# Fused cross-attention and feed-forward layer: a row of query factors through DRAM in place of four matmuls a batch, and the positions made ahead of x's low halves

## The chip, the cores and the metric

One core of a Trainium2 chip runs the whole kernel. The metric is the device time of one execution in microseconds (us), as a median over runs; lower is better.

## What is computed

```python
def _layernorm(x, axis=-1, eps=1e-05):
    ...
    x = x + _L0_xattn_ref(_layernorm(x, axis=-1), ctx_1024, ctx_1024, mask, fside, Wq, bq, Wk, bk, Wv, bv, Wo, bo)
    x = x + _L0_ffn_ref(_layernorm(x, axis=-1), W1, W2, ln_g, ln_b, router_W, router_b, raw_U, raw_V, gamma)
...
    q = _split_heads(Q @ Wq.T + bq)
    k = _split_heads(K @ Wk.T + bk)
    v = _split_heads(V @ Wv.T + bv)
    scores = jnp.einsum('bhqd,bhkd->bhqk', q, k) / jnp.sqrt(jnp.float32(DK))
    scores = jnp.where(mask == 0, jnp.float32(-1000000000.0), scores)
    scores = scores + attn_bias
    probs = jax.nn.softmax(scores, axis=-1)
```

Batch 8, 512 tokens of 512 features for x and for the context, 16 heads of 32, hidden width 2048, all float32. The mask is int32, 512x512 a batch.

## The kernel before

The kernel has three stages, each a block with a program of its own for each engine: `project` (L131) makes queries, keys, values and positions of all eight batches and splits the feed-forward weights, `attend` (L513) does the attention, `blend` (L875) the rest. At the end of a block all engines meet. The change is in `project` alone, which covers about the first 312 of 1888 us.

To keep precision at the fast rate of the matmul, each matrix is kept as a high half (rounded) and a low half (what is left), and each product is three passes (`PASSES`, L26), so one output tile of 128x512 takes 4 chunks x 3 passes = 12 matmuls of 128x512. A batch has 12 such products: four for k, four for v, four for q. They go through four PSUM banks (`ps_j`, `NPB = 4`), in this order on TensorE (L467 to L508): four k products, then 16 transposes of the normalised x (`xn`) into three banks (`ps_t`; the fourth group of four reuses the first bank and waits until VectorE has made the low half of the first, `xT_low`, L490), then four v products, then four small matmuls that spread the query factors over all partitions, then four q products. Each k product of the next batch reuses the bank of a q product, and waits until VectorE has read that (`bank_free`, L471).

The query factor is, for each query token, -1/sqrt(32), or 0 where the token's whole row of the mask is 0. VectorE makes the positions (1e9 where the mask is 0, L381), their minimum over each row (L384), and from it `q_fac` (L388): 128 partitions x 4. The q tiles have features on the partitions and tokens along the row, so the factors are wanted as a row of 512 that is the same on all partitions. Before, VectorE spreads each column to 128x128 (`fac_cols`, L392), TensorE multiplies these by the identity (L503) into a bank of its own (`ps_f`), and ScalarE copies that to `fac_row` (L450), which L410 reads when it moves q out of PSUM with bias and factor.

VectorE's order in a batch: statistics of x (L363, L367, L369), `xn` (L372, with `rstd` from GpSimd, L330), the four low halves `xT_l` (L376, each after ScalarE's high half, L445), positions, minimum, `q_fac`, `fac_cols`, four v tiles (L399), the low half of the next context (L356), four q tiles (L410).

SyncE issues all loads and stores of the stage on one queue, in the order of L263 to L299, and each wait holds back everything behind it: the feed-forward weights, the next context and x, the store of k, the store of the positions, the next mask, v, q, and the split weights. GpSimd makes the low half of the weights (L334, L339) and `rstd`. In batch 0 it does one such pass more, for the output projection's weights (L334).

Of the kernel before, what the change touches and what calls it, by code (L numbers as in the profile page):

```python
# [17 lines left out]
P = 128  # L18
# [25 lines left out]
def build(nc, x, ctxT, bias, mask, WqT, bq, WkT, bk, WvT, bv, WoT, bo, W1T, W2T,  # L44
          ln_g, ln_b, rWT, rb, rawU, rawV, gamma, out):

    q_d, k_d = (nc.dram_tensor(n, (NC * B, P, S), F32, kind="Internal").ap() for n in ("q_d", "k_d"))
    v_d = nc.dram_tensor("v_d", (NC * B, S, P), F32, kind="Internal").ap()
    pos_d = nc.dram_tensor("pos_d", (B, S, S), F32, kind="Internal").ap()
    att_d = nc.dram_tensor("att_d", (NC * B, P, S), F32, kind="Internal").ap()  # L50
    wo_d = nc.dram_tensor("wo_d", (2, P, NC * D), F32, kind="Internal").ap()
    wf_d = nc.dram_tensor("wf_d", (NF, P, 4, D), F32, kind="Internal").ap()

    with ExitStack() as top:
        ident = top.enter_context(nc.sbuf_tensor("ident", [P, P], F32))
        ones = top.enter_context(nc.sbuf_tensor("ones", [P, P], F32))
        neg_half = top.enter_context(nc.sbuf_tensor("neg_half", [P, NT], F32))
        ahead = Ahead(nc, top)
        project(nc, ident, ones, neg_half, x, ctxT, mask, WqT, bq, WkT, bk, WvT, bv, W1T, W2T,
                q_d, k_d, v_d, pos_d, wf_d, bias, WoT, wo_d, ahead)  # L60
        kept = Kept(nc, top)
        attend(nc, ident, bias, q_d, k_d, v_d, pos_d, att_d, x, wo_d, bo, rawU, rawV, kept, ahead)
        blend(nc, ident, ones, neg_half, x, att_d, ln_g, ln_b, rWT, rb, gamma, wf_d, kept, ahead, out)
# [65 lines left out]


def project(nc, ident, ones, neg_half, x, ctxT, mask, WqT, bq, WkT, bk, WvT, bv, W1T, W2T,  # L131
            q_d, k_d, v_d, pos_d, wf_d, bias, WoT, wo_d, ahead):
    NPJ = 3 * NC
    NPB = 4
    NTB = 3
    with ExitStack() as ctx:
        def sb(name, shape, dt=F32):
            return ctx.enter_context(nc.sbuf_tensor("p_" + name, shape, dt))

        def sem(name):  # L140
            return ctx.enter_context(nc.semaphore("p_" + name))
# [13 lines left out]
        pos = sb("pos", [P, NT, S])  # L155
        pos_min = sb("pos_min", [P, NT])
        q_fac = sb("q_fac", [P, NT])
        fac_cols = sb("fac_cols", [P, NT, P])
        fac_row = sb("fac_row", [P, S])
        bq_c, bk_c = sb("bq_c", [P, NC]), sb("bk_c", [P, NC])  # L160
        bv_r = sb("bv_r", [P, D])
# [5 lines left out]

        ps_t = ctx.enter_context(nc.psum_tensor("p_ps_t", [P, NTB, S], F32))
        ps_j = ctx.enter_context(nc.psum_tensor("p_ps_j", [P, NPB, D], F32))
        ps_f = ctx.enter_context(nc.psum_tensor("p_ps_f", [P, S], F32))  # L170

        consts_made = sem("consts_made")
        consts_zeroed = sem("consts_zeroed")
# [1 line left out]
        x_in, c_in, m_in = sem("x_in"), sem("c_in"), sem("m_in")  # L175
        kw_in, vw_in, qw_in = sem("kw_in"), sem("vw_in"), sem("qw_in")
        w_high, w_low = sem("w_high"), sem("w_low")
        pos_done, min_done, fac_done, cols_done = sem("pos_done"), sem("min_done"), sem("fac_done"), sem("cols_done")
        stats_done, mv_done, var_done, rstd_done, xn_done = (
            sem("stats_done"), sem("mv_done"), sem("var_done"), sem("rstd_done"), sem("xn_done"))  # L180
        x_turned, xT_high, xT_low = sem("x_turned"), sem("xT_high"), sem("xT_low")
        cT_high, cT_low = sem("cT_high"), sem("cT_low")
        fac_turned, fac_row_done = sem("fac_turned"), sem("fac_row_done")
        wf_in, wf_high, wf_low, wf_out = sem("wf_in"), sem("wf_high"), sem("wf_low"), ahead.wf_out
        wo_in, wo_high, wo_low, wo_out = sem("wo_in"), sem("wo_high"), sem("wo_low"), sem("wo_out")
        projected, bank_free = sem("projected"), sem("bank_free")
# [22 lines left out]
        def _(sp):  # L209
# [53 lines left out]
            def body(b, more):  # L263
                if b > 0:
                    sp.wait_ge(wf_low, b)
                    load_ff(b)
                if b >= B - 3:
                    load_ahead(b - (B - 3))
                if more:
                    sp.wait_ge(cT_low, b + 1)  # L270
                    load_c(b + 1)
                    sp.wait_ge(xn_done, NT * (b + 1))
                    load_x(b + 1)
                sp.wait_ge(k_done, NC * (b + 1))
                store_qk(b, k_s, k_d, k_out)
                sp.wait_ge(pos_done, b + 1)
                sp.dma_start(tokens(pos_d[b]), pos[:, :, :]).then_inc(pos_out, 16)
                if more:
                    load_m(b + 1)
                if b == 0:  # L280
                    sp.wait_ge(wo_low, 1)
                    store_wo()
                    load_ff(b)
                sp.wait_ge(bank_free, NPB + NVQ * b + NT)
                for c in range(NC):
                    sp.dma_start(tokens(v_d[B * c + b]), v_s[:, :, c * P:(c + 1) * P]).then_inc(v_out, 16)
                if more:
                    sp.wait_ge(bank_free, NPB + NVQ * (b + 1))
                    store_qk(b, q_s, q_d, q_out)
                else:  # L290
                    for c in range(NC):
                        if c == NC // 2:
                            sp.wait_ge(wf_low, b + 1)
                            store_ff(b)
                        sp.wait_ge(bank_free, NPB + NVQ * b + NT + c + 1)
                        sp.dma_start(q_d[B * c + b], q_s[:, c, :]).then_inc(q_out, 16)
                if more:
                    sp.wait_ge(wf_low, b + 1)
                    store_ff(b)  # L299
# [45 lines left out]
        def _(dve):  # L345
# [13 lines left out]
            def body(b, more):  # L359
# [11 lines left out]
                for t in range(NT):  # L371
                    dve.tensor_scalar(xn[:, t, :], x_raw[:, t, :], mv[:, t, 0:1], rstd[:, t:t + 1],  # L372
                                      ALU.subtract, ALU.mult).then_inc(xn_done, 1)
                for c in range(NC):
                    dve.wait_ge(xT_high, NC * b + c + 1)
                    dve.tensor_tensor(out=xT_l[:, c, :], in0=ps_t[:, c % NTB, :], in1=xT_h[:, c, :].bitcast(F32),  # L376
                                      op=ALU.subtract).then_inc(xT_low, 1)

                dve.wait_ge(m_in, 16 * b + 16)
                dve.wait_ge(pos_out, 16 * (b + 1))  # L380
                dve.tensor_scalar(pos[:, :, :], m_raw[:, :, :], 0.0, MASKED, ALU.is_equal, ALU.mult) \  # L381
# [5 lines left out]

                dve.tensor_scalar(q_fac[:, :], pos_min[:, :], 0.0, QSCALE, ALU.is_equal, ALU.mult) \  # L388
                    .then_inc(fac_done, 1)
                dve.wait_ge(fac_done, b + 1)  # L390
                for t in range(NT):
                    dve.tensor_scalar(fac_cols[:, t, :], ones[:, :], q_fac[:, t:t + 1], None, ALU.mult) \  # L392
                        .then_inc(cols_done, 1)
                for t in range(NT):
                    n = V_AT + t
                    dve.wait_ge(projected, NPJ * b + n + 1)
# [3 lines left out]
                        .then_inc(bank_free, 1)  # L400
                if more:
                    context_low(b + 1)
                dve.wait_ge(fac_row_done, b + 1)
                for c in range(NC):

                    n = Q_AT + c
# [16 lines left out]
        def _(act):  # L423
# [9 lines left out]
            def body(b, more):  # L433
# [12 lines left out]
                if more:  # L446
                    act.wait_ge(projected, NPJ * b + V_AT + NT)
                    context_high(b + 1)
                act.wait_ge(fac_turned, b + 1)
                act.activation(fac_row[:, :], ps_f[:, :], ACT.Copy).then_inc(fac_row_done, 1)  # L450
                act.wait_ge(wf_in, 64 * (b + 1))
                act.wait_ge(wf_out, 64 * (b + 1))
                act.wait_ge(wo_out, 32)
# [10 lines left out]
        def _(pe):  # L464
            pe.wait_ge(consts_made, 3)

            def body(b, more):  # L467
# [29 lines left out]
                for t in range(NT):  # L497
                    ts = slice(t * P, (t + 1) * P)
                    product(V_AT + t, [(a[:, k, ts], w[:, k, :]) for k in range(NC)
                                       for a, w in ((cT_h, w_h[2]), (cT_h, w_l[2]), (cT_l, w_h[2]))])  # L500
                pe.wait_ge(cols_done, NT * (b + 1))
                for t in range(NT):
                    last = pe.matmul(ps_f[:, t * P:(t + 1) * P], fac_cols[:, t, :], ident[:, :], start=True, stop=True)  # L503
                last.then_inc(fac_turned, 1)
                pe.wait_ge(w_low, 3)
                pe.wait_ge(xT_low, NC * (b + 1))
                for c in range(NC):
# [1030 lines left out]
```

## Time and profile before

| | us |
|---|---|
| median of 3 runs | 1891.92 (1888.12 to 1892.15) |
| profiled execution | 1890.4 |
| its span | 1888.5 |
| TensorE busy | 1818.5 (96%) |
| VectorE / ScalarE / GpSimd busy | 1037.1 / 793.8 / 888.1 |
| DMA queue of SyncE | 50.7% of 16 engines' span |

The span is what the trace covers; the execution lies 1.9 us above it. Times in the trace are us from the span's start. Rows of an engine's timeline give start, length, engine, line, operation, output<-inputs, and in brackets how long the engine sat idle before and what released it. PE is TensorE, DVE VectorE, ACT ScalarE, POOL GpSimd, SPq SyncE's queue. A matmul's length overlaps the next one's; from start to start, two matmuls of 128x512 are some 0.23 us apart.

### The profile page before, as it was taken

What the parts mean: (1) busy time and instruction counts of PE and PEld (TensorE: products, weight loads), DVE (VectorE), ACT (ScalarE), POOL (GpSimd) and SP (SyncE); (2) the same over time, 40 slices, a digit from 0 to 9 for tenths busy, and PEclk for the clock granted to TensorE, in tenths of its full rate; (3) what the DMA queues carried; (4) which work ended last, traced back from release to release, by engine and by line L of the source; (5) the groups of instructions that cost most, each with busy time, mean ns of one, the idle gap of its engine ahead of it and who ended that gap; (6) DMA issues with size and microseconds to landing.
All of it is one profiled execution on the core that took longest, in us unless ns stands there. A gap on an engine that the chain in (4) does not pass through costs nothing.

```text
span 1888.5 us, 31571 instructions
## 1 busy us (share of the span) xinstructions
PE 1818.5 (96%) x11736; PEld 1358.6 (72%) x11736; DVE 1037.1 (55%) x2401; ACT 793.8 (42%) x1720; POOL 888.1 (47%) x702
## 2 busy tenths in 40 slices
PE   6999998999999999999699999999999999999998
PEld 5888886555555555555477888888888888888886
DVE  5555555998998999899654422433233342332411
ACT  3222223888888888888331211312112131221310
POOL 1211214999999999999213232232322413223211
PEclk9999998999999999999889999999999999999999
DMA  8888888626245335431433463554535555355453
GB/s 298 286 302 313 311 314 310 244 96 224 91 135 178 137 115 174 147 115 36 143 116 101 150 213 123 179 189 163 195 122 189 188 170 190 121 198 177 150 188 114
DMA packets 198007, 340.11 MB, mean 180 GB/s; under 512 B 10464, under 2 KB 52064, under 8 KB 197344
## 3 DMA queue, kind: packets, MB, share of 16 engines
q1 hardware_dynamic: 194592, 325.50, 50.7%
q0 software_dynamic: 3264, 12.58, 1.9%
q8 instruction: 96, 1.57, 0.3%
q14 instruction: 55, 0.45, 0.1%
HBM read 268.84 MB, written 69.21 MB: 179 GB/s over the span
## 4 chain that ended last, share of the span: by engine, by line
PE 49%; DVE 2%; ACT 1%; issue 0%; POOL 0%; DVEq 0%; ACTq 0%
PE n_ps_y L1459 18%; PE n_ps_h L1440 18%; PE n_ps_m L1376 9%; PE n_ps_y L1376 2%; PE n_ps_m L1370 1%; DVE n_aT_l L1080 0%; DVE h_bias L1180 0%; DVE n_stats L1093 0%; DVE h_k L1180 0%; DVE h_bias L1152 0%; DVE n_g_h L1234 0%; DVE k_az L1105 0%; DVE k_x L1226 0%; DVE h_k L1161 0%; POOL n_rstd L1043 0%
## 5 line engine op out<-in xcount | busy, mean ns | idle before, releaser
L1062 POOL TENSOR_TENSOR n_g_l<-h_pos,n_g_h 128x512 fp32r<-128x512 f32 x128 | 186.4, 1456 | 581.3 <-DVE n_g_h L1234 581.3
L863 ACT ACTIVATE a_t_s<-a_t_s,a_nmax 128x512 f32<-128x512 f32 x512 | 364.4, 715 | 15.8 <-DVE a_nmax L812 15.8
L1440 PE MATMUL n_ps_h<-n_zT_h,n_w 128*128 128x512 f32 x1024 | 338.5, 392 | 2.1 <-DVE n_r_row L1210 2.1
L812 DVE CUSTOM_DVE_ANT_0 a_t_s<-a_ps_s,a_t_s 128x512 f32<-128x512 f32 x464 | 295.2, 687 | 44.8 <-PE a_ps_s L722 27.9
L733 PEld LDWEIGHTS a_ps_t<-ident,a_t_s 128*128 128x128 f32 x2048 | 221.3, 142 | 136.7 <-issue 108.8
L694 POOL TENSOR_TENSOR a_t_s<-a_pos,a_bias_t 128x512 f32<-128x512 f32 x256 | 317.8, 1271 | 0.2
L1459 PE MATMUL n_ps_y<-n_w,n_g_h 128*128 128x512 f32 x1024 | 316.6, 390 | 0.0
L1332 ACT ACTIVATE h_pos<-n_ps_h 128x512 f32<-128x512 f32 x128 | 75.5, 596 | 535.4 <-PE n_ps_h L1440 535.4
L733 PE MATMUL a_ps_t<-ident,a_t_s 128*128 128x128 f32 x2048 | 281.6, 281 | 0.3 <-ACT a_pT L850 0.3
L1234 DVE CAST n_g_h<-h_pos 128x512 fp32r<-128x512 f32 x128 | 55.8, 436 | 374.2 <-ACT h_pos L1332 374.2
L1440 PEld LDWEIGHTS n_ps_h<-n_zT_h,n_w 128*128 128x128 f32 x1024 | 193.3, 189 | 42.5 <-DVE n_r_row L1210 2.5
L1459 PEld LDWEIGHTS n_ps_y<-n_w,n_g_h 128*128 128x128 f32 x1024 | 191.2, 188 | 39.0
L1440 PE MATMUL n_ps_h<-n_zT_l,n_w 128*128 128x512 f32 x512 | 200.1, 391 | 0.0
L1459 PE MATMUL n_ps_y<-n_w,n_g_l 128*128 128x512 f32 x512 | 199.4, 389 | 0.0
L850 ACT ACTIVATE a_pT<-a_ps_t 128x512 f32<-128x512 f32 x256 | 151.4, 592 | 75.1 <-PE a_ps_t L733 75.0
L819 DVE COPY a_pT<-a_ps_t 128x512 f32<-128x512 f32 x256 | 164.3, 683 | 1.8 <-PE a_ps_t L733 1.8
L722 PE MATMUL a_ps_s<-h_k,h_q 32*128 32x512 f32 x1024 | 147.0, 643 | 16.5 <-DVE a_nmax L812 10.1
L747 PE MATMUL a_ps_o<-a_pT,a_v 128*32 128x256 f32 x2048 | 149.9, 388 | 0.0
L339 POOL TENSOR_TENSOR p_wf_l<-p_wf,p_wf_h 128x2048 fp32r<-128x2048 f32 x8 | 37.0, 4624 | 186.0 <-ACT p_wf_h L454 186.0
L694 POOL TENSOR_TENSOR a_t_s<-a_pos,h_bias 128x512 f32<-128x512 f32 x96 | 119.6, 1270 | 0.0
L1440 PEld LDWEIGHTS n_ps_h<-n_zT_l,n_w 128*128 128x128 f32 x512 | 96.7, 189 | 19.9
L1459 PEld LDWEIGHTS n_ps_y<-n_w,n_g_l 128*128 128x128 f32 x512 | 96.1, 188 | 20.1
(165 smaller groups left out, 2652.1 us busy)
## 6 DMA issues: line engine op xcount, KB each, us to landing
n_w<-wf_d SPq DMA_DIRECT2D x256, 512.0 KB, 4.2
a_pos<-pos_d SPq DMA_DIRECT2D x24, 1024.0 KB, 6.3
a_bias_t<-in_bias POOLq DMA_DIRECT2D x9, 1024.0 KB, 7.2
p_c_raw<-in_ctxT SPq DMA_DIRECT2D x8, 1024.0 KB, 8.0
p_x_raw<-in_x SPq DMA_DIRECT2D x8, 1024.0 KB, 10.3
p_m_raw<-in_mask SPq DMA_DIRECT2D x8, 1024.0 KB, 12.7
k_d<-p_k_s SPq DMA_DIRECT2D x8, 1024.0 KB, 12.1
pos_d<-p_pos SPq DMA_DIRECT2D x8, 1024.0 KB, 10.5
```

What stands on the lines that cost most here:

```text
L694: pool.tensor_tensor(out=t_s[:, j % NN, i:i + 1, :], in0=pos_rows(b, qt, qt + 1), in1=bias_rows(i, i + 1, qt), op=ALU.subtract).then_inc(n ...
L722: pe.matmul(ps_s[:, i, :], q[rows, b, qt * P:(qt + 1) * P], k[rows, b, :], start=True, stop=True).then_inc(scored, 1)
L733: last = pe.transpose(ps_t[:, BANK[i], kt * P:(kt + 1) * P], t_s[:, at[1] % NN, i, kt * P:(kt + 1) * P], ident[:, :])
L747: last = pe.matmul(ps_o[rows, :], v[:, b, kt, rows], pT[:, h, i, kt, :], start=kt == 0, stop=kt == NT - 1)
L812: dve.tensor_tensor_reduce(t_s[:, j % NN, i:i + 1, :], ps_s[:, i:i + 1, :], added, 1.0, 3.0e38, ALU.add, ALU.min, nmax[:, j % NN, i:i + 1] ...
L819: dve.tensor_copy(dst, src).then_inc(kept_dve, 1)
L850: act.activation(dst, src, ACT.Copy).then_inc(kept_act, 1)
L863: act.activation(t_s[:, j % NN, i, :], t_s[:, j % NN, i, :], ACT.Exp, scale=-1.0, bias=nmax[:, j % NN, i:i + 1], accum_out=total[:, j // 2 ...
L1062: pool.tensor_tensor(out=g_l[:, f % NG, :], in0=g_f[:, f % NG, :], in1=g_h[:, f % NG, :].bitcast(F32), op=ALU.subtract).then_inc(g_low, 1)
L1376: last = pe.matmul(dst, stationary, moving, start=start and n == 0, stop=stop and n == len(passes) - 1)
L1440: last = pe.matmul(ps_h[:, f % 2, :], stationary, moving, start=i == 0, stop=i == len(passes) - 1)
L1459: last = pe.matmul(ps_y[:, t, :], gs[i], w2[:, f % NW, j, :], start=f == 0 and m == 0, stop=f == NF - 1 and m == 2)
```

## The change

The factors go to DRAM and come back. A tensor `fac_d` (8 x 512) is added. SyncE stores `q_fac` into it, 512 single elements of 4 bytes, waits for that store, and loads the row of 2 KB to all 128 partitions as `fac_row`. `fac_cols`, its four VectorE operations, the four matmuls, the bank `ps_f` and ScalarE's copy go. On VectorE the positions, the minimum and `q_fac` come ahead of `xT_l`. On SyncE the positions' store, the factor store and the next mask's load come ahead of the store of k, and the factor load, with its waits, behind it.

```diff
@@ tensors of project
-        fac_cols = sb("fac_cols", [P, NT, P])
-        ps_f = ctx.enter_context(nc.psum_tensor("p_ps_f", [P, S], F32))
...
@@ SyncE, body of a batch
                     load_x(b + 1)
+                sp.wait_ge(pos_done, b + 1)
+                sp.dma_start(tokens(pos_d[b]), pos[:, :, :]).then_inc(pos_out, 16)
+                sp.wait_ge(fac_done, b + 1)
+                sp.dma_start(fac_d[b].rearrange("(t p) -> p t", p=P), q_fac[:, :],
+                             allow_slow_non_contiguous=True).then_inc(fac_out, 16)
+                if more:
+                    load_m(b + 1)
                 sp.wait_ge(k_done, NC * (b + 1))
                 store_qk(b, k_s, k_d, k_out)
-                sp.wait_ge(pos_done, b + 1)
-                sp.dma_start(tokens(pos_d[b]), pos[:, :, :]).then_inc(pos_out, 16)
-                if more:
-                    load_m(b + 1)
+                sp.wait_ge(fac_out, 16 * (b + 1))
+                sp.wait_ge(bank_free, NPB + NVQ * b)
+                sp.dma_start(fac_row[:, :], fac_d[b].rearrange("(a n) -> a n", a=1).broadcast_to([P, S])) \
+                    .then_inc(fac_in, 16)
                 if b == 0:
@@ VectorE, body of a batch
                                       ALU.subtract, ALU.mult).then_inc(xn_done, 1)
-                for c in range(NC):
-                    dve.wait_ge(xT_high, NC * b + c + 1)
-                    dve.tensor_tensor(out=xT_l[:, c, :], in0=ps_t[:, c % NTB, :], in1=xT_h[:, c, :].bitcast(F32),
-                                      op=ALU.subtract).then_inc(xT_low, 1)
-
                 dve.wait_ge(m_in, 16 * b + 16)
...
                     .then_inc(fac_done, 1)
-                dve.wait_ge(fac_done, b + 1)
-                for t in range(NT):
-                    dve.tensor_scalar(fac_cols[:, t, :], ones[:, :], q_fac[:, t:t + 1], None, ALU.mult) \
-                        .then_inc(cols_done, 1)
+                for c in range(NC):
+                    dve.wait_ge(xT_high, NC * b + c + 1)
+                    dve.tensor_tensor(out=xT_l[:, c, :], in0=ps_t[:, c % NTB, :], in1=xT_h[:, c, :].bitcast(F32),
+                                      op=ALU.subtract).then_inc(xT_low, 1)
+
...
-                dve.wait_ge(fac_row_done, b + 1)
+                dve.wait_ge(fac_in, 16 * (b + 1))
@@ ScalarE, body of a batch
-                act.wait_ge(fac_turned, b + 1)
-                act.activation(fac_row[:, :], ps_f[:, :], ACT.Copy).then_inc(fac_row_done, 1)
@@ TensorE, body of a batch
-                pe.wait_ge(cols_done, NT * (b + 1))
-                for t in range(NT):
-                    last = pe.matmul(ps_f[:, t * P:(t + 1) * P], fac_cols[:, t, :], ident[:, :], start=True, stop=True)
-                last.then_inc(fac_turned, 1)
```

VectorE's order from `xn` to the v tiles, the same in each batch. Before:

```order
L372 TENSOR_SCALAR p_xn<-p_x_raw,p_mv,p_rstd 128x512 x3
L376 TENSOR_TENSOR p_xT_l<-p_ps_t,p_xT_h 128x512 [waits p_xT_high] x4
L381 TENSOR_SCALAR p_pos<-p_m_raw 128x2048 [waits p_pos_out,p_m_in]
L384 TENSOR_REDUCE p_pos_min<-p_pos 128x4 [waits p_pos_done]
L388 TENSOR_SCALAR p_q_fac<-p_pos_min 128x4 [waits p_min_done]
L392 TENSOR_SCALAR p_fac_cols<-ones,p_q_fac 128x128 [waits p_fac_done]
L392 TENSOR_SCALAR p_fac_cols<-ones,p_q_fac 128x128 x3
L399 TENSOR_TENSOR p_v_s<-p_ps_j,p_bv_r 128x512 [waits p_v_out,p_projected]
```

Now (line numbers are those of the changed kernel):

```order
L378 TENSOR_SCALAR p_xn<-p_x_raw,p_mv,p_rstd 128x512 x3
L382 TENSOR_SCALAR p_pos<-p_m_raw 128x2048 [waits p_pos_out,p_m_in]
L385 TENSOR_REDUCE p_pos_min<-p_pos 128x4 [waits p_pos_done]
L389 TENSOR_SCALAR p_q_fac<-p_pos_min 128x4 [waits p_min_done]
L393 TENSOR_TENSOR p_xT_l<-p_ps_t,p_xT_h 128x512 [waits p_xT_high] x4
L401 TENSOR_TENSOR p_v_s<-p_ps_j,p_bv_r 128x512 [waits p_v_out,p_projected]
```

The four low halves moved behind three operations on the mask, and `fac_cols` is gone.

SyncE's queue in a batch, from the next x to the first v store. Before:

```order
L222 DMA p_x_raw<-in_x 128x4x512 [waits p_xn_done]
L231 DMA k_d<-p_k_s 128x4x512 [waits p_k_done]
L277 DMA pos_d<-p_pos 128x4x512 [waits p_pos_done]
L228 DMA p_m_raw<-in_mask 128x4x512
L286 DMA v_d<-p_v_s 128x4x128 [waits p_bank_free]
```

Now:

```order
L221 DMA p_x_raw<-in_x 128x4x512 [waits p_xn_done]
L274 DMA pos_d<-p_pos 128x4x512 [waits p_pos_done]
L276 DMA fac_d<-p_q_fac 128x4x1 [waits p_fac_done]
L227 DMA p_m_raw<-in_mask 128x4x512
L230 DMA k_d<-p_k_s 128x4x512 [waits p_k_done]
L284 DMA p_fac_row<-fac_d 128x512 [waits p_bank_free,p_fac_out]
L292 DMA v_d<-p_v_s 128x4x128 [waits p_bank_free]
```

Two transfers were added, and the second one's wait for the first stands ahead of the v stores.

## Rows read from the trace of the kernel before

**Rows 1.** Busy time by engine, window of batch 5: stretch, us, engines, PEclk, DMA share, GB/s
```profile
209.00:245.00 36.00, 35.32 (x168) 29.39 (x167) 19.67 (x33) 9.02 (x11) 5.63 (x2) 1.00 0.98 347
```
**Rows 2.** Waits in the stage: engine, line, for whom: us, times, longest
```profile
PE p_ps_t L493 <- DVE p_xT_l L376: 5.1, 8, 0.7
```
**Rows 3.** Timeline of TensorE and ScalarE, batch 2, around the factor matmuls
```profile
117.14 1.05 PE L503 MATMUL p_ps_f<-ident,p_fac_cols 128*128 128x128 f32 x8
...
117.95 0.48 PE L477 MATMUL p_ps_j<-p_xT_h,p_wq_h 128*128 128x512 f32 x1
...
128.95 0.39 PE L477 MATMUL p_ps_j<-p_cT_h,p_wk_h 128*128 128x512 f32 x1
```
**Rows 4.** Timeline of VectorE, batch 2
```profile
97.86 1.92 DVE L372 TENSOR_SCALAR p_xn<-p_x_raw,p_mv,p_rstd 128x512 f32<-128x512 f32 x4 [1.12 <-POOL p_rstd L330]
...
104.97 1.88 DVE L376 TENSOR_TENSOR p_xT_l<-p_ps_t,p_xT_h 128x512 fp32r<-128x512 f32 x3 [5.20 <-ACT p_xT_h L445]
...
107.66 1.22 DVE L381 TENSOR_SCALAR p_pos<-p_m_raw 128x2048 f32<-128x2048 int32 x1
...
111.23 0.17 DVE L388 TENSOR_SCALAR p_q_fac<-p_pos_min 128x4 f32<-128x4 f32 x1
...
121.50 0.74 DVE L410 SCALAR_TENSOR_TENSOR p_q_s<-p_ps_j,p_bq_c,p_fac_row 128x512 f32<-128x512 f32 x1
...
129.15 0.75 DVE L410 SCALAR_TENSOR_TENSOR p_q_s<-p_ps_j,p_bq_c,p_fac_row 128x512 f32<-128x512 f32 x1 [1.97 <-PE p_ps_j L477]
```
**Rows 5.** Timelines of VectorE, GpSimd and TensorE in batch 0; last, window as in rows 1
```profile
28.02 1.91 DVE L372 TENSOR_SCALAR p_xn<-p_x_raw,p_mv,p_rstd 128x512 f32<-128x512 f32 x4 [1.22 <-POOL p_rstd L330]
31.36 1.89 DVE L376 TENSOR_TENSOR p_xT_l<-p_ps_t,p_xT_h 128x512 fp32r<-128x512 f32 x3 [1.42 <-ACT p_xT_h L445]
...
30.92 4.57 POOL L334 TENSOR_TENSOR p_wf_l<-p_wf,p_wf_h 128x2048 fp32r<-128x2048 f32 x1 [2.94 <-ACT p_wf_h L442]
...
29.99 1.80 PE L493 MATMUL p_ps_t<-ident,p_xn 128*128 128x128 f32 x12 [3.46 <-DVE p_xn L372]
32.10 1.12 PE L493 MATMUL p_ps_t<-ident,p_xn 128*128 128x128 f32 x4 [0.31 <-DVE p_xT_l L376]
...
32.00:34.60 2.60, 2.50 (x8) 2.21 (x9) 1.96 (x5) 1.02 (x2) 2.60 (x1) 0.51 0.86 216
```
**Rows 6.** Timelines of VectorE and GpSimd in batch 1
```profile
60.34 1.29 DVE L369 TENSOR_SCALAR p_var_e<-p_mv 128x4 f32<-128x4 f32 x1
...
56.96 4.64 POOL L339 TENSOR_TENSOR p_wf_l<-p_wf,p_wf_h 128x2048 fp32r<-128x2048 f32 x1 [21.47 <-ACT p_wf_h L454]
```
**Rows 7.** Mask loads, batches 2, 5, 6: SyncE's timeline, DMA issues with us to landing
```profile
109.31 0.70 SPq L228 DMA_DIRECT2D p_m_raw<-in_mask  x1
...
p_m_raw<-in_mask SPq DMA_DIRECT2D x1, 1024.0 KB, 11.6
...
220.62 1.14 SPq L228 DMA_DIRECT2D p_m_raw<-in_mask  x1
...
p_m_raw<-in_mask SPq DMA_DIRECT2D x1, 1024.0 KB, 15.2
...
254.38 2.78 SPq L228 DMA_DIRECT2D p_m_raw<-in_mask  x1
```
**Rows 8.** Three small loads at the start, the same two views
```profile
2.63 0.74 SPq L304 DMA_DIRECT2D p_bq_c<-in_bq  x1
3.41 0.49 SPq L305 DMA_DIRECT2D p_bk_c<-in_bk  x1
3.94 0.46 SPq L306 DMA_DIRECT2D p_bv_r<-in_bv  x1
...
p_bv_r<-in_bv SPq DMA_DIRECT2D x1, 256.0 KB, 10.0
...
p_bq_c<-in_bq SPq DMA_DIRECT2D x1, 2.0 KB, 9.2
p_bk_c<-in_bk SPq DMA_DIRECT2D x1, 2.0 KB, 8.8
```

More of the change, by code:

```diff
@@ L51, in build @@
     wo_d = nc.dram_tensor("wo_d", (2, P, NC * D), F32, kind="Internal").ap()
+    fac_d = nc.dram_tensor("fac_d", (B, S), F32, kind="Internal").ap()
     wf_d = nc.dram_tensor("wf_d", (NF, P, 4, D), F32, kind="Internal").ap()
@@ L59, in build @@
         project(nc, ident, ones, neg_half, x, ctxT, mask, WqT, bq, WkT, bk, WvT, bv, W1T, W2T,
-                q_d, k_d, v_d, pos_d, wf_d, bias, WoT, wo_d, ahead)
+                q_d, k_d, v_d, pos_d, wf_d, bias, WoT, wo_d, fac_d, ahead)
         kept = Kept(nc, top)
@@ L131, in project @@
 def project(nc, ident, ones, neg_half, x, ctxT, mask, WqT, bq, WkT, bk, WvT, bv, W1T, W2T,
-            q_d, k_d, v_d, pos_d, wf_d, bias, WoT, wo_d, ahead):
+            q_d, k_d, v_d, pos_d, wf_d, bias, WoT, wo_d, fac_d, ahead):
     NPJ = 3 * NC
@@ L177, in project @@
         w_high, w_low = sem("w_high"), sem("w_low")
-        pos_done, min_done, fac_done, cols_done = sem("pos_done"), sem("min_done"), sem("fac_done"), sem("cols_done")
+        pos_done, min_done, fac_done = sem("pos_done"), sem("min_done"), sem("fac_done")
         stats_done, mv_done, var_done, rstd_done, xn_done = (
@@ L182, in project @@
         cT_high, cT_low = sem("cT_high"), sem("cT_low")
-        fac_turned, fac_row_done = sem("fac_turned"), sem("fac_row_done")
+        fac_out, fac_in = sem("fac_out"), sem("fac_in")
         wf_in, wf_high, wf_low, wf_out = sem("wf_in"), sem("wf_high"), sem("wf_low"), ahead.wf_out
```

## The prediction

> **What bounds the kernel now.** The change touches the first stage only, so I read first the busy time in windows of one batch. In batch 5 TensorE works 35.32 of 36.00 us at full clock [rows 1]; the other batches look the same, with a lower DMA share than this one's 0.98. The table of waits then shows where the little that is missing lies: TensorE waits eight times, once a batch, for VectorE's first low half ahead of the fourth group of transposes, 5.1 us in all [rows 2]. So the stage is TensorE's line of work plus that wait. A matmul removed from the line counts in full, and anything that makes VectorE or a DMA late counts as soon as its slack is gone. The timelines of the engines [rows 3 to 6] and the landing times of the transfers [rows 7, 8] give those slacks. What follows the stage keeps its length and only moves with it.
>
> **What is removed.** On TensorE the factor matmuls start at 117.14 and the first q product at 117.95 [rows 3]: 0.81 us a batch, on the line, in all eight batches: **-6.5 us**. ScalarE's copy and the four `fac_cols` go as well; neither engine is waited for there, so they count nothing.
>
> **Positions ahead of the low halves, batches 1 to 7.** From the start of the positions to the end of `q_fac` VectorE needs 111.40 - 107.66 = 3.7 us [rows 4]. In batch 2 `xn` is finished at 99.78, and the first low half starts only at 104.97, after 5.2 us of idleness. The moved work would end at 103.5: 1.4 us of slack, cost 0. The work that hides it is the k products. What it was a cover for, the time under the v products, is idle afterwards. The mask has landed long before, since its load is issued a batch earlier.
>
> **The same in batch 0.** Here TensorE itself waits for `xn` (3.46 us) and there is no cover: `xn` ends at 29.93 and the low half starts at 31.36 [rows 5]. Positions and minimum take until about 33.5. Then `q_fac` meets GpSimd, which works on the output weights from 30.92 to 35.49 [rows 5]. The trace shows what a small VectorE operation of this kind does beside that: `var_e`, 128x4 like `q_fac`, starts at 60.34 and ends at 61.63, where GpSimd's ends at 61.60 [rows 6]; the `q_fac` of the same form takes 0.17 alone [rows 4]. So I take it that `q_fac` ends when GpSimd does; GpSimd itself starts some 0.2 us late, since the positions hold it up in the same way, so at about 35.8. The low half then starts at 35.95 instead of 31.36: 4.6 us that TensorE stands still, where the lower end is 2.3 (`q_fac` not held: 29.93 + 3.8 = 33.7) and the upper 7.8 (GpSimd comes first and holds the positions too, which then start at 35.5 and give the low half at 39.2). I take 4.6, being nearest to what `var_e` shows. Behind the first pause the granted clock was 0.51 over 2.6 us [rows 5], which lost 1.3 us; a second pause loses between nothing and that much again, I take 0.7. Nothing in the batches after has slack on TensorE that would swallow it. **+5.3 us** (2.3 to 9.1).
>
> **The factors through DRAM.** SyncE issues the store behind x and the positions, then mask and k, and waits for the store before it issues the load. The load is queued behind 2 MB, mask and k, which take the place of k, positions and mask of before, so the last of them lands when the mask landed before, plus what the new store takes in the queue. There is no row for a store of 512 elements of 4 bytes. Nearest are two loads of 128 rows of 16 bytes, of which the second lands at 3.41 + 8.8 = 12.2, 0.4 us after the first at 11.8; four times as many make **1.5 us**. The lower end is 0. The upper end comes from the load of one row to 128 partitions, which lands at 13.9, 1.7 us after that [rows 8]: at that price 512 pieces are 6.9 us. I take 1.5, since that row's pieces are small too. The Trainium skill ("DMA: Bandwidth & Descriptors", Specifications) says that transfers below 512 bytes miss the line rate and are done as read-modify-write; it gives no price for a piece, and by it the store would be dearer than those loads, which no row here shows. The factor load has the shape of that 2 KB row to 128 partitions: 1.7 us.
>
> When must it be there? The k product of the next batch starts at 128.95 [rows 3] and needs the bank of the first q tile, 0.75 us of VectorE; less the 0.81 that goes, the row must land by 127.4 in the old times of batch 2. VectorE wants it at 121.50 already, but the later q tiles only come out of TensorE until 129.15 [rows 4], so it catches up. The mask landed at 109.31 + 11.6 = 120.9; plus 3.2 gives 124.1: **3.3 us of slack, cost 0**. In batch 5 two more megabytes are in the queue. The mask landed at 220.62 + 15.2 = 235.8, the row lands at 239.0, and the limit, 108.8 us further on (three batches of 36.27), is 236.2: TensorE waits **2.8 us**. Batch 6: 254.38 + 15.2 = 269.6, row at 272.8, limit 272.5: **0.3 us** [rows 7]. The last batch has no next k product. Together +3.1 us (0.3 with a free store and a load of 0.7). SyncE's wait for the store also holds the v stores back: little in most batches, 4 to 5 us in batch 5; their buffer is wanted again 20 us later, so that counts nothing. The k store is issued later by two transfers, and ScalarE reuses its buffer 25 us later: nothing. In batch 0 the feed-forward weights behind the added wait come some 3 us later, less than the 4.5 us by which all else there is moved.
>
> **Sum.** -6.5 + 5.3 + 3.1 = **+1.9 us** on the profiled execution's own 1890.4 (span 1888.5), that is 1892.3. The median of the runs lies 1.5 above that execution, so the forecast is **1893.8 us**: no change that can be told, since a measurement here separates about 0.2%, 3.8 us.
>
> **Rivals.**
> *The small store is dear (slower).* Mechanism: 512 pieces of 4 bytes clog the queue, the row lands after the limit, and the next k product waits for its bank. For it: batch 5 is already over its limit and batch 6 at it, and the pieces are a quarter the size of the nearest row's; against it: batch 2 has 3.3 us left. The sum passes +3.8 once the store takes more than 2.5 us (each us beyond 1.5 costs 2, in batches 5 and 6). At 4 us the waits are 5.3 + 2.8, the sum +6.9, 1898.8. At 6.9, with batches 1 to 4 taken as batch 2, 4 x 2.1 + 8.2 + 5.7 = 22.3, the sum +21 and 1913. Chance 0.29, time 1899. The read-modify-write of the Trainium skill's page named above would act in this way.
> *GpSimd wins the race in batch 0 (slower).* The positions start after it, 7.8 instead of 4.6: sum +5.1, 1897.0. It needs GpSimd to start 1 us earlier than its row, so 0.10.
> *Both costs are small (faster).* `q_fac` is not held, the clock costs nothing more, store and load are nearly free: -6.5 + 2.3 + 0.3 = -3.9, 1888.0. For it: minimum and `q_fac` touch four numbers a partition; against it: `var_e`. Chance 0.17.
> That the change does nothing on TensorE can be left out: the eight gaps of 0.81 us hold matmuls and no wait.
>
> **How the numbers follow.** Forecast 0.44; the rivals 0.29, 0.10 and 0.17. Slower is then 0.39, faster 0.17, within 0.2% 0.44. The range from 1887 reaches a little below the faster case and to 1908 above, into the dear store's stretch of 1896 to 1913, of which the last part is left out. The forecast's own range is 1890 to 1896.
>
> **What would show it.** Right: the q products start 0.23 us after the last v matmul; in batch 0 the fourth transposes start near 36.7 and `q_fac` ends with GpSimd's operation; in batches 1 to 4 TensorE has no wait but the old 0.7 us; in batch 5 it waits for VectorE's first q tile 2 to 4 us, and VectorE for the factor load. Wrong: waits for that load in every batch (store too cheap in my sum), none in batch 5 (too dear), or low halves late in batches 1 to 7.

## The result, and the profile after

The changed kernel takes 1918.11 us (median of 4 runs, 1914.08 to 1920.7), the kernel before, run beside it, 1891.24 (1888.12 to 1892.15): the ratio is 1.0142, 95% interval 1.0129 to 1.0154. It is slower by 26.9 us; the forecast was 1893.8, and the range ended at 1908. The profiled execution took 1914.08 us, the fastest of the four, with a span of 1912.3 us at a granted clock of 0.985; against the profile of before it is 23.7 us longer, and these 23.7 us are what the following accounts for. The other 3.2 us between the medians lie outside the two profiled executions, and no trace shows them.

The whole difference arises in the first stage. The first matmul of `attend` starts at 312.81 before and at 336.37 now, 23.6 us later; from there to the end both take 1576 us. The busy time by engine over the stage, of before and of after:

```profile
0.00:312.81 312.81, 288.31 (x1344) 239.16 (x1345) 166.31 (x267) 81.18 (x93) 50.52 (x25) 0.99 0.86 302
```

```profile
0.00:336.37 336.37, 287.04 (x1280) 234.96 (x1281) 162.97 (x235) 77.38 (x85) 52.22 (x25) 0.96 0.98 286
```

The last two columns are the ones to read. The DMA queue was busy for 0.86 of 312.8 us, 269 us; now for 0.98 of 336.4, 330 us, and it moves fewer GB/s. The store of 2 KB and the load of the row have together brought about 60 us of queue time, and the queue had 44 us to spare (312.8 - 269). The table of waits over the stage (engine, line, for whom: us, times, longest), which answers to [rows 2]:

```profile
DVE p_q_s L412 <- DMA p_fac_row<-fac_d: 56.7, 7, 13.4
PE p_ps_j L477 <- DVE p_q_s L412: 15.7, 6, 8.1
PE p_ps_t L493 <- DVE p_xT_l L393: 11.0, 8, 4.3
PE a_ps_s L718 <- PEq L137: 5.3, 1, 5.3
```

VectorE waits for the row in seven batches of eight, and TensorE then for a bank in six: 1.0, 0.5, 2.0, 1.9, 8.1 and 2.2 us by its timeline. SyncE's timeline in batch 2 (start, length) and the DMA issues with their us to landing answer to [rows 7]; VectorE's row stands at the end:

```profile
112.41 0.51 SPq L221 DMA_DIRECT2D p_x_raw<-in_x  x1
112.95 0.69 SPq L274 DMA_DIRECT2D pos_d<-p_pos  x1
113.69 1.80 SPq L276 DMA_DIRECT2D fac_d<-p_q_fac  x1
115.53 2.60 SPq L227 DMA_DIRECT2D p_m_raw<-in_mask  x1
131.01 0.33 SPq L284 DMA_DIRECT2D p_fac_row<-fac_d  x1
...
p_x_raw<-in_x SPq DMA_DIRECT2D x1, 1024.0 KB, 9.3
pos_d<-p_pos SPq DMA_DIRECT2D x1, 1024.0 KB, 16.2
p_m_raw<-in_mask SPq DMA_DIRECT2D x1, 1024.0 KB, 17.4
p_fac_row<-fac_d SPq DMA_DIRECT2D x1, 256.0 KB, 5.0
fac_d<-p_q_fac SPq DMA_DIRECT2D x1, 2.0 KB, 17.3
...
136.06 2.73 DVE L412 SCALAR_TENSOR_TENSOR p_q_s<-p_ps_j,p_bq_c,p_fac_row 128x512 f32<-128x512 f32 x4 [6.21 <-DMA p_fac_row<-fac_d]
```

x lands at 112.41 + 9.3 = 121.7. A megabyte at about 400 GB/s, the rate of the microseconds before, takes 2.6 us, so the positions should be in DRAM at 124.3. They land at 129.15 and the factors at 113.69 + 17.3 = 131.0, so the store costs 131.0 - 124.3 = 6.7 us of queue time. The same stretch by windows of 2 us (the last two columns are DMA share and GB/s):

```profile
122.00:124.00 2.00, 2.00 (x10) 1.67 (x9) 0.69 (x1) 0.00 (x0) 0.00 (x0) 1.00 1.08 356
124.00:126.00 2.00, 2.00 (x10) 1.65 (x10) 0.39 (x1) 0.39 (x1) 0.00 (x0) 1.00 1.37 194
126.00:128.00 2.00, 2.00 (x11) 1.65 (x10) 0.74 (x2) 2.00 (x2) 0.00 (x0) 1.00 1.05 128
```

The 16 DMA engines count as busy as ever and move half, then a third as much. (The share adds up the whole length of each packet that starts in the window, so it can pass 1.00.) Batch 0, by the timelines of VectorE, GpSimd and TensorE, answers to [rows 5]:

```profile
33.67 2.17 DVE L389 TENSOR_SCALAR p_q_fac<-p_pos_min 128x4 f32<-128x4 f32 x1
35.75 1.87 DVE L393 TENSOR_TENSOR p_xT_l<-p_ps_t,p_xT_h 128x512 fp32r<-128x512 f32 x3
...
31.30 4.51 POOL L340 TENSOR_TENSOR p_wf_l<-p_wf,p_wf_h 128x2048 fp32r<-128x2048 f32 x1 [3.08 <-ACT p_wf_h L444]
...
36.48 1.11 PE L493 MATMUL p_ps_t<-ident,p_xn 128*128 128x128 f32 x4 [4.27 <-DVE p_xT_l L393]
```

That is the forecast to 0.2 us. Batch 1, the same engines, answers to [rows 6] and was not forecast:

```profile
64.11 4.62 POOL L345 TENSOR_TENSOR p_wf_l<-p_wf,p_wf_h 128x2048 fp32r<-128x2048 f32 x1 [28.30 <-ACT p_wf_h L454]
...
64.97 3.79 DVE L375 TENSOR_SCALAR p_var_e<-p_mv 128x4 f32<-128x4 f32 x1
...
76.11 1.12 PE L493 MATMUL p_ps_t<-ident,p_xn 128*128 128x128 f32 x4 [2.67 <-DVE p_xT_l L393]
```

SyncE waits for the factor store until 48.27 before it issues the first feed-forward weights. GpSimd's pass over them runs at 64.11, 7.15 us later than before, and now lies on the whole of `var_e`, which takes 3.79 us in place of 1.29. GpSimd can make `rstd` only behind that pass, at 68.84, so `xn` starts at 69.89; the positions, the minimum and `q_fac` stand between `xn` and the first low half, which starts at 75.38.

At the end of the stage VectorE waits for the last batch's row, so that batch's q tiles come late, their stores with them, and the block cannot end:

```profile
328.21 2.07 DVE L412 SCALAR_TENSOR_TENSOR p_q_s<-p_ps_j,p_bq_c,p_fac_row 128x512 f32<-128x512 f32 x3 [7.28 <-DMA p_fac_row<-fac_d]
```

SyncE issues the first q stores only at 328.99, and behind them the split weights and the last q stores until 335.66. TensorE, whose last product ends at about 331, waits 5.3 us for the end of the block. Before it was 2.4 (from the table of waits of before):

```profile
PE a_ps_s L722 <- PEq L136: 2.4, 1, 2.4
```

### The profile page after: what moved, and what is told of

Its sections match the earlier page's. It is cut to its first block, busy times and chain, and to the rows that moved or that the text cites. A ratio compares the mean times of both kernels' runs of the same rounds, so it can differ in the third digit from the quotient of the medians.

```text
span 1912.3 us, 31427 instructions
## 1 busy us (share of the span) xinstructions
PE 1817.4 (95%) x11672; PEld 1354.0 (71%) x11672; DVE 1033.4 (54%) x2369; ACT 790.5 (41%) x1712; POOL 889.9 (47%) x702
## 4 chain that ended last, share of the span: by engine, by line
PE 48%; DVE 2%; ACT 1%; issue 0%; POOL 0%; DVEq 0%; ACTq 0%
PE n_ps_y L1455 18%; PE n_ps_h L1436 18%; PE n_ps_m L1372 9%; PE n_ps_y L1372 2%; PE n_ps_m L1366 1%; DVE n_aT_l L1076 0%; DVE h_bias L1176 0%; DVE n_stats L1089 0%; DVE h_k L1176 0%; DVE h_bias L1148 0%; DVE n_g_h L1230 0%; DVE n_zT_l L1106 0%; DVE k_az L1101 0%; DVE k_x L1222 0%; DVE h_k L1157 0%
## 6 DMA issues: line engine op xcount, KB each, us to landing
p_m_raw<-in_mask SPq DMA_DIRECT2D x8, 1024.0 KB, 17.6
```

## The experiments

The first four take the change apart. All ratios are to the kernel before, run on the same chip, with 95% intervals.

**e1: the same store in 128 pieces of 16 bytes.** A partition's four words go side by side, so the factors stand in another order in the row.

```diff
-sp.dma_start(fac_d[b].rearrange("(t p) -> p t", p=P), q_fac[:, :],
-             allow_slow_non_contiguous=True).then_inc(fac_out, 16)
+sp.dma_start(fac_d[b].rearrange("(p t) -> p t", p=P), q_fac[:, :]).then_inc(fac_out, 16)
```

> The changed kernel with the factor store as 128 pieces of 16 bytes (one a partition) in place of 512 pieces of 4 bytes; the row read back then has its factors in another order, nothing else differs. Theory A (the number of pieces fills the queue: some 6.5 us for 512): the store lands within 2 to 3 us of where the positions' store would have, the later waits for the row shrink to batches 5 and 6, and the time falls by some 18 us from the changed kernel's, to 1891 to 1897. Rival B (the store's size is nothing; the round trip through SyncE, with the load issued only after it behind 2 MB, makes the row late): 1912 or more, within 4 us of the changed kernel.

Measured: 1889.79 us, ratio 0.999 (0.998 to 0.9999). Every byte is still stored, waited for and read back, and the whole loss is gone; the time even lies a little under the 1891 to 1897 that I expected. DMA issues in batch 2, and the waits of the stage:

```profile
p_x_raw<-in_x SPq DMA_DIRECT2D x1, 1024.0 KB, 9.4
fac_d<-p_q_fac SPq DMA_DIRECT2D x1, 2.0 KB, 12.2
```

```profile
PE p_ps_j L476 <- DVE p_q_s L411: 1.4, 1, 1.4
```

x is issued at 107.01 and lands at 116.4, the factors at 108.11 + 12.2 = 120.3. Less 2.6 us for the positions, the store costs 1.3 us, about the 1.5 that my forecast had for the other one.

The wait for the store is still there, and what it held up is not late. GpSimd's pass in batch 1 and TensorE's wait at the end of the block:

```profile
57.68 4.62 POOL L344 TENSOR_TENSOR p_wf_l<-p_wf,p_wf_h 128x2048 fp32r<-128x2048 f32 x1 [22.14 <-ACT p_wf_h L453]
PE a_ps_s L717 <- PEq L137: 2.1, 1, 2.1
```

The store lands 5.6 us after its issue in batch 0 (35.60, 41.23), where the changed kernel's takes 12.4 (35.87, 48.27). The pass is 0.7 us later than before, and TensorE's wait for the low half in batch 1 is 0.68 as before.

**e2: no store, the row loaded from `bv`.** The factors in q are replaced by bv.

```diff
-sp.wait_ge(fac_done, b + 1)
-sp.dma_start(fac_d[b]..., q_fac[:, :], ...).then_inc(fac_out, 16)
...
-sp.wait_ge(fac_out, 16 * (b + 1))
-sp.dma_start(fac_row[:, :], fac_d[b]...)
+sp.dma_start(fac_row[:, :], bv...)
```

> The changed kernel without the factor store and without SyncE's wait for it; the row is loaded from the bias of v instead, with the same shape and at the same place of the queue, so q is scaled by other numbers. Both theories: the row lands with the k store, about 2 us behind it, no TensorE wait for it but in batch 5 (up to 1 us); what is left is the removed matmuls (-6.5) and batch 0 (+5.3): 1889 to 1893, ratio to before 0.999 to 1.001. If it stays more than 5 us above before, the load or the new order of the queue costs by itself.

Measured: 1889.03, ratio 0.9986 (0.9976 to 0.9995), 0.8 us below e1. The row's load costs nothing that can be told in the time. The queue is busy for 0.88 x 309.6 = 272 us, some 3 more than before and 57 less than in the changed kernel.

**e3: positions, minimum and factors back behind the low halves,** the rest as changed (the `xT_l` loop moved up again).

> The changed kernel with the positions back behind x's low halves on VectorE; factors still through DRAM. Theory A: batch 0 gives back its 4.4 us at the fourth transposes and what the clock lost, and batch 1 its 2 us; the queue of SyncE is so deep that a store that is issued 5 to 8 us later still lands at about the same time, so the waits for the row stay: 6 to 8 us below the changed kernel, 1909 to 1913. Rival B: every microsecond by which the store is issued later makes the row later; 3 to 5 us more in each of seven batches: 1930 or more.

Measured: 1930.76, ratio 1.0209 (1.0188 to 1.0231). Batch 0 gets its 5 us back, and the kernel is still some 13 us slower than the changed one (1.0209 against 1.0142).

```profile
DVE p_q_s L412 <- DMA p_fac_row<-fac_d: 75.9, 8, 13.4
PE p_ps_j L477 <- DVE p_q_s L412: 25.4, 7, 8.2
PE p_ps_t L493 <- DVE p_xT_l L382: 4.7, 7, 0.7
```

My theory's figure was too low, the rival's holds: the place of the positions counts as well. In batch 2 the positions are issued 6.1 us behind x (117.71, 123.79), where the changed kernel issues them 0.5 us behind it.

**e4: the kernel before with the positions ahead only,** four matmuls a batch kept.

> The kernel before with only VectorE's order changed: positions, minimum, q_fac and fac_cols ahead of x's low halves, the factor matmuls kept. By the prediction's term for batch 0 it costs 5.3 us (here with fac_cols, 0.9 us more: up to 6.2), and nothing in batches 1 to 7: 1896 to 1899, ratio 1.0025 to 1.004. Rival: the pause in batch 0 belongs to the store and its queue and not to the order: within 1 us of before.

Measured: 1897.54, ratio 1.0029 (1.0018 to 1.0039), 5.9 us slower. TensorE in batch 0; in the other batches its wait stays at 0.68:

```profile
37.06 1.12 PE L493 MATMUL p_ps_t<-ident,p_xn 128*128 128x128 f32 x4 [4.36 <-DVE p_xT_l L391]
```

So the store is dear. Why, when its pieces are only four times as many as the loads' that I took as its price? The next two put a store that nobody waits for into the kernel before, in the same place: from `neg_half`, 128x4, once to neighbouring words and once with 512 bytes from each piece to the next.

```diff
 sp.dma_start(tokens(pos_d[b]), pos[:, :, :]).then_inc(pos_out, 16)
+sp.dma_start(fac_d[b].rearrange("(t p) -> p t", p=P), neg_half[:, :], ...)              # e5
+sp.dma_start(fac_d[b].rearrange("(t p) n -> p t n", p=P)[:, :, 0], neg_half[:, :], ...)  # e6
```

**e5**

> The kernel before with one thing added: behind each store of the positions SyncE stores 512 pieces of 4 bytes, from a constant tile (128 x 4), to 512 neighbouring words of DRAM, and nothing waits for it. Theory A (the pieces themselves take some 6.5 us of all queues): the mask's load, which stands right behind it, lands 6 to 7 us later than before (17 to 19 us after issue in batches 1 to 4 in place of 11.6 to 13.5), at a data rate far below the 300 GB/s around it. Rival (the store is only late because the positions' store ahead of it and the wait delay it): the mask lands within 1 us of before. The time itself stays within 4 us of before, since the pauses of the queue take most of it up.

**e6**

> As the dense bystander, but each 4 byte piece goes to a place of its own, 512 bytes from the next. If a piece costs by being a piece, the mask is as late as with the dense one (6 to 7 us). If neighbouring words written by different queues get in each other's way, it is late by less than 2 us.

Measured: e5 1900.16, ratio 1.005 (1.0035 to 1.0065); e6 1891.91, ratio 1.0001 (0.9991 to 1.0011). The windows of e5, then of e6:

```profile
122.00:124.00 2.00, 2.00 (x11) 1.65 (x11) 0.03 (x1) 0.00 (x0) 0.00 (x0) 1.00 1.06 387
124.00:126.00 2.00, 2.00 (x15) 1.78 (x14) 0.69 (x1) 1.95 (x2) 0.00 (x0) 1.00 1.71 203
126.00:128.00 2.00, 2.00 (x11) 1.64 (x10) 2.00 (x1) 2.00 (x2) 0.00 (x0) 1.00 0.84 81
```

```profile
120.00:122.00 2.00, 2.00 (x11) 1.65 (x10) 2.00 (x2) 1.31 (x1) 0.61 (x1) 1.00 1.11 331
122.00:124.00 2.00, 2.00 (x11) 1.65 (x10) 0.53 (x2) 0.00 (x0) 2.00 (x1) 1.00 0.56 169
124.00:126.00 2.00, 2.00 (x11) 1.65 (x10) 0.22 (x1) 0.00 (x0) 2.00 (x1) 1.00 0.01 3
```

The number and the size of the pieces are the same, in the trace too: up to 320 us, 7086 packets under 512 bytes in e5, 7168 in e6, 2944 before. With neighbouring words the queue crawls at 81 GB/s; with 512 bytes between them it has finished about when it did before the store was there: the mask lands after 10.9 us in batch 2, with neighbouring words after 16.3, before after 11.6 [rows 7]. What is dear is not a 4-byte piece but 4-byte pieces right beside each other.

The trace's records of single packets, which no view prints, show where the time goes. A piece of 4 bytes takes 9 ns in e5 as in e6. The 2 KB packets of the large transfers grow: most take 84 to 95 ns, but in e5 247 of them take more than 1 us over the stage, in the changed kernel 282, in e6 7 and before 2. In e5 the pieces of batch 2 go out between 123 and 125 us, and the 29 packets of 2 KB that start from 125 to 126 take 0.93 us on average.

My expectation that e5 would stay within 4 us of before failed: it is 9.7 us slower by the medians. Its stage ends 6.2 us later, and most of that is batch 1, where TensorE waits 5.3 us for `xn`: GpSimd's pass there starts at 64.88, 7.9 us later than before, although inside the stage nothing waits for the store.

**e9: does the store cost because it is waited for?** The changed kernel with its store, but the row comes from `bv` and SyncE's wait for the store is gone (VectorE waits for the store of the batch before ahead of a new `q_fac`, and all stores are waited for at the end of the stage).

> The changed kernel with its store of the factors as it is, but the row is loaded from bv, so nobody reads what was stored (the factors in q are replaced by bv), and SyncE waits for the store nowhere in a batch. Theory A (the round trip costs: the load can only be issued when the store has landed, and v stores and feed-forward weights stand behind that wait): the row is issued straight after the k store, so it lands within 2 us of k, at about +22 us from the positions' issue in batch 2 (135), the bank waits shrink from 15.7 to 3 us or less, total 1892 to 1898. Rival B (the store's own time in the queue costs, whoever waits): k still lands as late as in the changed kernel (22 us behind the positions' issue), the row with it, bank waits 8 us or more, total 1908 to 1918.

Measured: 1921.53, ratio 1.016 (1.0147 to 1.0173), no faster than the changed kernel and above the range of rival B too. Theory A falls. The row is issued at 124.97, straight behind k, and lands at 141.0, because the queue in front of it is slow (DMA issues, batch 2):

```profile
fac_d<-p_q_fac SPq DMA_DIRECT2D x1, 2.0 KB, 17.7
k_d<-p_k_s SPq DMA_DIRECT2D x1, 1024.0 KB, 18.4
p_fac_row<-in_bv SPq DMA_DIRECT2D x1, 256.0 KB, 16.0
```

```profile
DVE p_q_s L414 <- DMA p_fac_row<-in_bv: 53.9, 7, 13.2
PE p_ps_j L479 <- DVE p_q_s L414: 18.9, 6, 8.0
```

The wait of the round trip is no part of the loss in the banks; the store's time ahead of the row is. The same holds for the two other losses. GpSimd's pass in batch 1 and the end of the block are as late as in the changed kernel, though SyncE waits for no factor store inside a batch and the v stores go out as soon as VectorE has made the tiles (325.32, against 325.29):

```profile
64.10 4.63 POOL L345 TENSOR_TENSOR p_wf_l<-p_wf,p_wf_h 128x2048 fp32r<-128x2048 f32 x1 [28.94 <-ACT p_wf_h L456]
PE a_ps_s L720 <- PEq L137: 5.0, 1, 5.0
```

**e10: e3 with the pieces of e1.**

> The changed kernel with positions, minimum and factors back behind the low halves, and the store in 128 pieces of 16 bytes (factors in another order in the row). It tells apart what made the positions' place cost so much in the run before that had them behind. Theory A (the late issue alone costs some 4 us a batch, the dear store the rest): the row lands 6 to 7 us earlier than with the dear store, bank waits 2 to 10 us in place of 25.4, total 1888 to 1900. Rival B (the late issue is enough by itself): bank waits over 15 us, total 1908 to 1922.

Measured: 1890.13, ratio 0.9991 (0.9983 to 1.0). Bank waits 1.7 us in place of 25.4. A late issue alone costs next to nothing; it costs only behind a queue that the dense store has filled. This settles e3.

**e11 and e12: how near is near?** Two stores that nobody waits for, as in e5: e11 in 128 pieces of 16 bytes, `"(p t) -> p t"`; e12 in 512 pieces of 4 bytes, 64 bytes apart.

> The kernel before plus a store nobody waits for, behind the positions: 128 pieces of 16 bytes, a partition's four words side by side, neighbours from other queues right beside them. Theory A (what is dear is the number of writes into the same small stretch of DRAM: 512 in 2 KB): a quarter of the dense store's effect or less, it lands within 3 us of the positions, mask at most 2 us later than before, total 1889 to 1894. Rival B (any writes closer together than 64 bytes from several queues are dear): lands 5 us or more behind the positions, total 1897 or more.

> The kernel before plus a store nobody waits for, behind the positions: 512 pieces of 4 bytes, each 64 bytes from the next. Theory A (pieces clash when they share one line of 64 bytes or less): costs as little as with 512 bytes between them, store lands near 10 us, no drop to about 80 GB/s, total 1889 to 1894. Rival B (pieces clash when they share a stretch of 512 bytes): store lands near 17 us, a drop to 80 to 130 GB/s behind it, total 1897 to 1903.

Measured: e11 1890.14, e12 1891.33, both at a ratio of 0.9998 (0.999 to 1.0007). The store lands after 11.6 and 10.3 us in batch 2, in e5 after 15.1. So 64 bytes between pieces are enough for the kernel's time. In the queue there are steps: the positions' store, which stands right ahead, lands after a median of 17.6 us in e5, 12.0 in e11, 11.2 in e12, 10.7 in e6 and 10.5 before, and 22 packets of 2 KB take more than 1 us in e11, 6 in e12. Whether the dear thing is many writes to one stretch of 64 bytes, or pieces that fill less than some smaller unit of it, stays open; the small step of the 16-byte pieces side by side does not tell them apart.

**Two versions that were to beat both kernels.** e7 keeps the factors' way through DRAM and gives each partition four neighbouring tokens in mask, positions and factors, so that pieces of 16 bytes come out in the right order; batch 0 keeps VectorE's old order.

```diff
-sp.dma_start(m_raw[:, :, :], tokens(mask[b]))
+sp.dma_start(m_raw[:, :, :], mask[b].rearrange("(p t) n -> p t n", p=P))
...
+if b == 0:
+    halves()        # else behind q_fac
```

> The changed kernel with a token order in which the factors of a partition are neighbours (partition p has rows 4p to 4p+3 of the mask, in its load, the positions, their store and the factor store), so the same result needs 128 pieces of 16 bytes; and in batch 0 alone x's low halves come ahead of the positions, as before. By theory A and the term for batch 0: -6.5 for the matmuls, 0 to +3 for the row in batches 5 and 6: 1885 to 1889 beside 1891.6, ratio 0.9965 to 0.9985. Rival (late issue matters most: in batch 0 the store is issued 5 us later, and then the row and the weights behind it are late): 1890 to 1893.

Measured: 1889.2, ratio 0.9994 (0.9985 to 1.0003), which can't be told from the kernel before and lies just above my range. Batch 0 is cured, batch 1 is not; TensorE's timeline:

```profile
31.33 0.66 PE L497 MATMUL p_ps_t<-ident,p_xn 128*128 128x128 f32 x4 [0.54 <-DVE p_xT_l L382]
66.48 1.53 PE L497 MATMUL p_ps_t<-ident,p_xn 128*128 128x128 f32 x12 [1.81 <-DVE p_xn L377]
70.73 0.66 PE L497 MATMUL p_ps_t<-ident,p_xn 128*128 128x128 f32 x4 [2.72 <-DVE p_xT_l L382]
```

The feed-forward weights still stand behind the store's wait, which ends at 41.19. In e1 the pause of batch 0 covers that; here nothing does, and `rstd`, behind GpSimd's pass, makes `xn` late.

e8 leaves DRAM out: from the kernel before, `fac_cols` becomes the identity with each row scaled by 0 or 1, in the rounded format, and one matmul of 128x512 by ones spreads it; ScalarE's copy puts the scale in.

```diff
-dve.tensor_scalar(fac_cols[:, t, :], ones[:, :], q_fac[:, t:t + 1], None, ALU.mult)
+dve.tensor_scalar(fac_cols[:, t, :], ident[:, :], q_fac[:, t:t + 1], None, ALU.mult)
...
-for t in range(NT):
-    last = pe.matmul(ps_f[:, t * P:(t + 1) * P], fac_cols[:, t, :], ident[:, :], ...)
+last = pe.matmul(ps_f[:, :], ones_r[:, :], fac_cols[...], ...)
```

> The kernel before, factors kept on TensorE, but spread by one matmul of 128x512 at the fast rate (a matrix of ones times the identity scaled by 0 or 1 a column, both exact; the factor -1/sqrt(32) is applied by ScalarE in its copy) in place of four 128x128 at the slow one. 0.23 us in place of 0.81 us a batch on the line of TensorE: -0.58 x 8 = -4.6 us, 1887 beside 1891.6, ratio 0.9975 (0.9965 to 0.9985). If it does nothing, the 0.81 us between v and q products was not bound by these matmuls.

Measured: 1885.65 (1883.76 to 1886.5), ratio 0.9971 (0.996 to 0.9981), 5 us faster than the kernel before. Busy time by operation:

```profile
L503 PE MATMUL p_ps_f<-p_fac_cols,p_ones_r 128*128 128x512 f32 x8 | 3.2, 396 | 0.0
```

Eight times 0.81 - 0.23 us are 4.6, and the medians differ by 4.9. It takes most of what the change was after and touches no queue.

## Why the prediction was wrong

The step that failed is the **price of the small store**: "four times as many make 1.5 us". It measured 6.7 in batch 2. Over the whole stage, the DMA share times its length is 0.98 x 336.4 = 329.7 us in the changed kernel and 272.4 in e2, which has no store: 57 us for eight stores, 7.2 each. Against e1 (0.90 x 311.9 = 280.7) it is 49 us, so the dense store costs 6.1 us more than one in pieces of 16 bytes; e5 against e6 gives 1.00 x 319.0 against 0.87 x 312.7 = 272.0, 5.9 each. The price lies near the upper bound of 6.9, which came from the load of one row to 128 partitions. The choice between the ends went by the size of the pieces, and the two loads it rested on differ from the store in what turned out to matter: their 16 bytes a partition lie together. They are loads, too, but e1's store has that shape and costs 1.3 us, near the 1.5 that I took. The page of the Trainium skill that I weighed ("DMA: Bandwidth & Descriptors", Specifications: transfers below 512 bytes are done as read-modify-write) pointed to the right side. As it stands it does not give the result, since e6 and e12 write pieces as small, and their time is that of the kernel before. So the bound came out near the price by luck: it is the price of another transfer, a row of 2 KB to each of 128 partitions, and no row ahead of the result showed what density does.

Term by term, on TensorE:

| | forecast | measured |
|---|---|---|
| factor matmuls | -6.5 | -6.5, gone from the timeline |
| batch 0, wait | +4.6 | +4.0 (4.27 against 0.31) |
| bank waits | +3.1 | +15.7 |
| batch 1, wait | 0 | +2.0 (2.67 against 0.68) |
| end of the block | 0 | +2.9 (5.3 against 2.4) |
| clock | +0.7 | +4.8 |

The sum of the measured column is 22.9 of the 23.6 us; 0.7 are not placed. The sign that I had set for "store too cheap in my sum", a wait for the row in every batch, came in seven of eight.

*Positions ahead, batches 1 to 7: nothing.* Right: outside batches 0 and 1 the wait for the low halves is 0.68 in both kernels, and e4 shows the whole move as 5.9 us, against 5.3 forecast. In batch 1 of the changed kernel the slack is gone, because `xn` comes late there (see the result).

*q_fac held by GpSimd in batch 0.* Right, 2.17 us in place of 0.17. The rival in which GpSimd comes first did not happen.

*Limits of the row.* The mechanism was right, and batch 5 was rightly named as the worst: the 8.1 us wait stands at the end of it. Its size follows from the store's price. The "small store is dear" rival gave 1913 at 6.9 us, a sum of +21 where the trace has +23.6, and that nearness is partly luck. It had 22.3 us of bank waits and the trace has 15.7: 5.4 for 8.4 in batches 1 to 4, 8.1 for 8.2 in batch 5, 2.2 for 5.7 in batch 6. It had too little for the three rows below, which make 9.7 where the forecast had 0.7. That the last batch has no next k product does not make its row harmless: the row holds the last q tiles, and those hold the end of the block.

*"Feed-forward weights some 3 us later, less than the 4.5 us."* Right for the store as I had priced it, wrong for this one. e1 keeps the wait, its GpSimd pass in batch 1 is 0.7 us later than before, and TensorE loses nothing there. With the dense store the pass is 7.15 us late, and just as late in e9, which does not wait. So this is the price of the store again, not of the wait. The bare wait shows only where batch 0 has no pause to cover it: TensorE's two waits in batch 1 of e7 are 4.5 us against 0.7 before, and the last bank wait 0.8. In e7's profiled execution (1885.16, the fastest of its eleven) the stage is 4.4 us shorter than before; its median is only 1.3 us lower, and no trace shows the rest.

*"v stores held back counts nothing."* Right. In the last batch SyncE stands at the factor store until 323.65 and issues the v stores at 324.03, some 3 us after the last v tile. But e9 issues them at once and waits 5.0 us at the end of the block all the same, and e1, with the wait, 2.1. What holds the end is the late row.

*Clock.* Of one pause I took 0.7. There were three, in batch 0, in batch 1 and behind batch 5, and in each the granted clock fell to 0.50, 1.2 GHz. Matmuls of 128x512 are then 0.43 us apart, not 0.23. The stretches at 0.50, first that of before, then the three of the changed kernel (TensorE's busy time stands behind the comma, the granted clock third from the end):

```profile
31.10:34.50 3.40, 3.09 (x12) 2.40 (x11) 2.50 (x5) 1.90 (x4) 3.40 (x1) 0.50 0.77 193
31.20:41.40 10.20, 5.93 (x20) 4.66 (x18) 7.05 (x7) 2.18 (x5) 4.51 (x1) 0.50 1.22 244
75.50:78.90 3.40, 2.79 (x9) 2.40 (x10) 2.45 (x4) 0.60 (x1) 0.00 (x0) 0.50 1.07 345
249.60:259.80 10.20, 4.04 (x10) 3.20 (x11) 4.94 (x8) 0.00 (x0) 0.00 (x0) 0.50 0.73 233
```

TensorE works 12.8 us at 0.50 there, before 3.1. The 9.7 us more would have taken half as long at full clock, so the clock cost 4.8 us. In the last stretch 4.0 us of work follow a wait of 8.15 us: half of these 4.0, 2.0 us, come on top of the wait. A stall costs more than its length.

The forecast's form failed, too: I priced each batch by whether the row met its limit, against slacks measured with the old queue. In a queue that is 86% busy, what a batch adds and doesn't fit is carried into the next; after the change every window from 90 us on (36 us each, the last 30) shows a share of 0.97 to 1.07 (300 GB/s at 1.00 from 90 to 126, before 0.84 and 292 GB/s). Adding eight times the bound, 55 us, to 269 gives 324, more than the stage's 313, and would have shown it at once.

## What to carry to other kernels

Before adding a transfer, set its queue time, at both ends of its price, against the queue's idle time over the stage: the sum tells when single slacks stop holding. Do not store single words side by side from 128 partitions in a queue that is nearly full; turn the layout so that a partition's words lie together, or leave 64 bytes between them. A late row costs also where nothing seems to follow it: in the last batch it held the last stores. And a wait on an in-order queue is paid for by what stands behind it. Here those were the next weights, and the price showed once no other pause covered it (e7).

## What the runs showed of the hardware

512 pieces of 4 bytes into one stretch of 2 KB took 6 to 7 us of all 16 engines' time and drew the traffic down to 81 to 203 GB/s, from 390. The same 512 pieces 64 or 512 bytes apart, and 128 of 16 bytes, left the kernel before at a ratio of 0.9998 to 1.0001. The slowness begins before the store lands: the positions ahead of it on the queue land 5 us late too. It does not show in the store's own packets, 9 ns each, but in the 2 KB packets beside and behind them, of which some 250 in the stage took more than 1 us, where most take 84 to 95 ns. What in the memory or on the way there makes this so, no run shows.
